# Normed tokens turned for the next pass: DMA transposes of two fp16 parts in place of TensorE transposes

## The chip, the cores and the metric

The kernel runs on one core of a Trainium2 chip. The metric is the device time of one execution in microseconds; the time of a version is the median of its runs. The engines are TensorE (PE, with its weight loads as PEld), VectorE (DVE), ScalarE (ACT), GpSimd (POOL) and SyncE (SP), whose queue issues all DMAs here.

## The reference

There are 64 graphs of 128 nodes with 512 features in fp32. Two masked attentions with 8 heads of 64 follow each other, then a feed-forward block and two more norms:

```python
eq, nk, nv = lin(x, n2e_q), lin(x, n2e_k), lin(x, n2e_v)
edges = ln(attn(eq, nk, nv, adj^T) + x, norm1)
nq, ek, ev = lin(x, e2n_q), lin(edges, e2n_k), lin(edges, e2n_v)
nodes = ln(x + attn(nq, ek, ev, adj), norm2)
h = gelu(lin(nodes, ffn_w1))                      # 512 -> 2048
y = ln(nodes + lin(h, ffn_w2), norm3)             # 2048 -> 512
out = layernorm(x + y)
```

attn(q, k, v, mask) is softmax(q k^T / 8 where the mask is above 0) v, head by head; ln(t, g, b) is (t - mean) / sqrt(var + 1e-5) * g + b over the 512 features.

## The kernel before

The work goes in groups of four graphs (GB = 4, 512 tokens). Attention makes two passes over 16 groups, groups 0 to 15 for the edges and 16 to 31 for the nodes; then the feed-forward pass goes over 16 groups. Every fp32 operand of a projection is held as a high and a low part (x_hi, x_lo), and a product is three matmuls.

A group of attention is four steps, u = 0 to 3. Each engine has its own program, written out by hand in `body(g, parity, before, own, after)`, and the engines meet through semaphores, each executing its list strictly in order. A step of the **PE** (L930 on) is: the keys and the queries of head pair u (24 matmuls), `weigh` of an earlier unit (40 small matmuls of turned probabilities with values, into `out_bank`), a block of values (12 matmuls), and the scores of the unit (12 matmuls). A *unit* is a head pair of the group, 8 score matrices of 128 x 128.

The softmax of a unit goes around DVE and ACT. DVE takes the maxima (`mask_and_maximum`, L760, 8 instructions), ACT the exponentials (`exponentials`, L520) and the high fp16 part (`probabilities_high`, L527), DVE the low part (`probabilities_low`, L769, two instructions), and SP turns both with two DMA transposes (`turn_probabilities`, L377 and L380). Behind p_lo DVE makes the low parts of keys and queries (L741, L744, L749), for which ACT made the high ones (L507 to L514), and then `add_weighed` (L684 to L706): the weighed values, divided by the row sums, are added to the residual tokens into `total[parity]` (L697), with the statistics of the norm (L702, and L706 once a group). Only then does DVE take the maxima of the next unit. Scores wait for q_lo.

**The end of a group's norm, where the change is.** When all four units of group g are added, POOL makes the inverse spread (`inverse_spread`, L608 and L610), and in the next group DVE centres the tokens in place at u = 2 (`centre`, L678, four instructions between v_rest and p_lo). The next pass needs the tokens with features on the partitions, times gain plus shift. So the PE transposes each graph's 128 x 512 tokens into the one bank `turn_bank` (`turn`, L837, four transposes against an identity matrix), and ACT copies it with gain and shift to `turned` (`copy_turned`, L477, four instructions), from where SP stores it (`store_turned`, L386). The four turns of group g-1 are spread over the steps: b = 0 and b = 1 at u = 2 (the second in the middle of a block of values), b = 2 at u = 3, b = 3 at u = 0 of the next group. A turn waits until ACT has copied the one before. In pass 2 the centred tokens are also stored as they are (`store_tokens`, L391).

POOL's list per group is: the middle and low parts of the values (`value_low`, L621 and L623, four times, each after DVE's v_rest of the block, L736), the low part of the next source (`split_source`, L636, four), the value bias onto the residual tokens (`add_bias`, L641, four), `inverse_spread`, and in pass 2 the low part of the next queries (`split_queries`, L630, four). SP's list per group has the loads (source, tokens, adjacency, in pass 2 queries), the eight transposes of probabilities, and the stores.

The first group of the feed-forward pass does the last group's turns: `attention["turn"]` and its fellows at chunks c = 8 to 11, with its weights loaded piece by piece meanwhile.

## Time and profile before

| | us |
|---|---|
| median of 3 runs | 2919.3 (2918.19 to 2920.08) |
| the profiled execution, its own time | 2920.29 |
| its span, first to last instruction | 2918.5 |
| PE busy / PEld busy | 2862.3 (98%) / 2396.2 |
| DVE busy | 1744.8 (60%) |
| ACT busy | 1551.6 (53%) |
| POOL busy | 1094.2 (37%) |
| mean granted PE clock, share of 2.4 GHz | 0.994 |

The shares are of the whole span, of which the attention passes take about the first half. In that half DVE and ACT are far busier than the mean says, since the feed-forward pass needs little of them. A chain of waits follows the last instruction back to what released it. A timeline gives start, duration, engine, line and operation; instructions of a kind that follow each other are merged with "xN", and an instruction that waits for a resource after it was started shows as a longer one.

### The profile page before, as it was taken

The page shows a single profiled execution, that of the slowest core. Times are in us where ns is not written, and L with a number is a line of the kernel's source. Part 1 is how long each engine was busy: PE and PEld are TensorE (multiplying, and loading weights), DVE is VectorE, ACT ScalarE, POOL GpSimd, SP SyncE. Part 2 cuts the span into 40 slices and gives each one's busy share as a digit, 9 for nine tenths or more (in the row PEclk, how much of TensorE's full clock was granted, in tenths as well). Part 3 has the DMA queues.
Part 4 walks back from the last instruction along what each step waited for, and adds up shares of the span by engine and source line. Part 5 has one row for each costly group of instructions (what it writes and reads, how often), then busy time and mean ns, then how long its engine had stood idle before and what let it go on. Part 6 is the DMA issues. An engine that isn't in the chain of part 4 may idle for free.

```text
span 2918.5 us, 50564 instructions
## 1 busy us (share of the span) xinstructions
PE 2862.3 (98%) x17920; PEld 2396.2 (82%) x17920; DVE 1744.8 (60%) x5684; ACT 1551.6 (53%) x4138; POOL 1094.2 (37%) x995
## 2 busy tenths in 40 slices
PE   9999999999999999999989999999999999999997
PEld 7888888888788888888868888888888888888886
DVE  7888888888888888888863233332233332233333
ACT  6777777777778787887854222222222222222221
POOL 3443434434355454654513322233321233321233
PEclk9999999999999999999999999999999999999998
DMA  7555555555567666766653110111110101110101
GB/s 200 121 123 124 123 121 120 115 132 119 139 164 173 161 167 161 180 172 162 163 146 122 58 53 34 43 43 57 57 57 29 52 34 57 57 57 29 67 6 58
DMA packets 488013, 296.08 MB, mean 101 GB/s; under 512 B 278912, under 2 KB 410112, under 8 KB 487808
## 3 DMA queue, kind: packets, MB, share of 16 engines
q1 hardware_dynamic: 487808, 293.49, 38.5%
q8 instruction: 111, 1.82, 0.2%
q14 instruction: 94, 0.77, 0.1%
HBM read 159.21 MB, written 67.11 MB: 78 GB/s over the span
## 4 chain that ended last, share of the span: by engine, by line
PE 94%; ACT 2%; DVE 2%; issue 1%; DMA 0%; SPq 0%; POOLq 0%; POOL 0%; DVEq 0%; ACTq 0%
PE proj L871 34%; PE proj L1320 24%; PE score L1334 12%; PE proj L1334 12%; PE score L922 6%; PE att_out L855 5%; PE att_turn L837 2%; ACT turned L477 1%; ACT att_probs L520 0%; DMA ffn_weight_raw<-in_w 0%; DVE normed L697 0%; DVE ffn_stats L1217 0%; DMA att_weight_v_raw<-in_n2e_v_w 0%; DVE att_p_lo L769 0%; DVE att_stats L702 0%
## 5 line engine op out<-in xcount | busy, mean ns | idle before, releaser
L1253 DVE TENSOR_TENSOR hidden_lo<-hidden,hidden_hi 128x512 fp32r<-128x512 f32 x256 | 186.9, 730 | 936.0 <-ACT hidden_hi L1105 936.0
L1112 ACT ACTIVATE hidden<-proj,ffn_bias 128x512 f32<-128x512 f32 x256 | 176.6, 690 | 996.7 <-PE proj L1320 996.6
L520 ACT ACTIVATE att_probs<-att_probs,att_minus_max 128x128 f32<-128x128 f32 x1024 | 397.3, 390 | 87.0 <-DVE att_minus_max L760 87.0
L769 DVE TENSOR_TENSOR att_p_lo<-att_probs,att_p_hi 128x512 f16<-128x512 f32 x256 | 212.3, 868 | 150.7 <-ACT att_p_hi L527 150.7
L1172 POOL TENSOR_TENSOR source_lo<-source_raw,source_hi 128x512 fp32r<-128x512 f32 x60 | 79.4, 1324 | 449.6 <-ACT source_hi L1123 449.6
L760 DVE CUSTOM_DVE_ANT_0 att_probs<-score,att_mask 128x128 f32<-128x128 f32 x1024 | 225.8, 285 | 34.7 <-PE score L922 34.2
L621 POOL CAST att_v<-att_v_rest 128x512 bf16<-128x512 f32 x128 | 95.6, 747 | 400.6 <-DVE att_v_rest L736 400.6
L477 ACT ACTIVATE turned<-att_turn,att_shift,att_gain 128x128 f32<-128x128 f32 x512 | 192.9, 458 | 69.9 <-PE att_turn L837 69.9
L871 PE MATMUL proj<-weight_v_hi,source_hi 128*128 128x512 f32 x512 | 216.4, 423 | 10.0 <-DVE weight_v_lo L718 7.2
L636 POOL TENSOR_TENSOR source_lo<-source_raw,source_hi 128x512 fp32r<-128x512 f32 x128 | 163.3, 1298 | 131.9 <-ACT source_hi L543 131.9
L871 PE MATMUL proj<-source_hi,weight_k_hi 128*128 128x512 f32 x512 | 201.6, 394 | 2.3 <-DVE weight_k_lo L718 2.3
L871 PE MATMUL proj<-weight_v_hi,source_lo 128*128 128x512 f32 x512 | 202.6, 396 | 0.0
L871 PE MATMUL proj<-weight_v_lo,source_hi 128*128 128x512 f32 x512 | 201.3, 393 | 0.0
L871 PE MATMUL proj<-source_lo,weight_k_hi 128*128 128x512 f32 x512 | 201.1, 393 | 0.0
L871 PE MATMUL proj<-source_hi,weight_k_lo 128*128 128x512 f32 x512 | 199.9, 390 | 0.0
L1320 PE MATMUL proj<-source_hi,w_lo 128*128 128x512 f32 x512 | 199.2, 389 | 0.0
L1320 PE MATMUL proj<-source_hi,w_hi 128*128 128x512 f32 x512 | 199.2, 389 | 0.0
L1320 PE MATMUL proj<-source_lo,w_hi 128*128 128x512 f32 x512 | 199.2, 389 | 0.0
L520 ACT ACTIVATION_READ_ACCUMULATOR att_probs<-att_probs,att_minus_max 128x1 f32 x1024 | 191.8, 187 | 0.0
L641 POOL TENSOR_TENSOR att_tokens<-att_tokens,bias_row 128x512 f32<-128x512 f32 x128 | 182.5, 1426 | 0.3 <-DMA att_tokens<-in_x 0.3
L855 PEld LDWEIGHTS att_out<-att_v,att_pt_hi 128*128 128x128 f16 x3072 | 149.0, 98 | 33.5 <-issue 33.2
L855 PE MATMUL att_out<-att_v,att_pt_hi 128*128 128x64 bf16 x3072 | 164.1, 193 | 0.0
(148 smaller groups left out, 8256.9 us busy)
## 6 DMA issues: line engine op xcount, KB each, us to landing
att_tokens<-in_x SPq DMA_DIRECT2D x128, 256.0 KB, 3.2
edges_t<-turned SPq DMA_DIRECT2D x64, 256.0 KB, 2.7
source_raw<-edges_t SPq DMA_DIRECT2D x16, 1024.0 KB, 6.0
att_query_raw<-in_x_t SPq DMA_DIRECT2D x16, 1024.0 KB, 7.5
nodes_t<-turned SPq DMA_DIRECT2D x64, 256.0 KB, 2.9
source_raw<-nodes_t SPq DMA_DIRECT2D x16, 1024.0 KB, 6.1
normed<-nodes SPq DMA_DIRECT2D x16, 1024.0 KB, 5.6
ffn_weight_raw<-in_x SPq DMA_DIRECT2D x16, 1024.0 KB, 8.1
```

Source lines behind the costliest of these rows:

```text
L477: last = nc.scalar.activation(turned[:, b % 2, c, :], turn_bank[:, c * P:(c + 1) * P], ACT.Identity, bias=shift_column[own][:, c:c + 1], s ...
L520: nc.scalar.activation(probs[:, j, :], probs[:, j, :], ACT.Exp, bias=minus_max[:, j:j + 1], scale=-1.0, accum_out=row_sum[:, side, j:j + 1 ...
L641: nc.gpsimd.tensor_tensor(pair(tokens, u), pair(tokens, u), bias_v[:, u * P:(u + 1) * P].rearrange("p (o d) -> p o d", o=1).to_broadcast([ ...
L760: nc.vector.tensor_tensor_reduce(out=probs[:, 4 * h + j, :], in0=score_bank[h][:, j * P:(j + 1) * P], in1=mask[:, 2 * h + j // 2, :], scal ...
L769: nc.vector.tensor_tensor(p_lo[:, 4 * h:4 * h + 4, :], probs[:, 4 * h:4 * h + 4, :], p_hi[:, 4 * h:4 * h + 4, :], ALU.subtract).then_inc(p ...
L855: last = nc.tensor.matmul(out, p, value, start=(i == 0), stop=(i == len(products) - 1))
L871: last = nc.tensor.matmul(bank[:], stationary, moving, start=(c == 0 and i == 0), stop=(c == C - 1 and i == 2))
L922: last = nc.tensor.matmul(score_bank[h][:, 2 * i * P:2 * (i + 1) * P].rearrange("p (s j) -> p s j", s=2), q, k, start=(n == 0), stop=(n == 2))
L1112: nc.scalar.activation(hidden[:, c % 2, :], up_bank[c % 2][:], ACT.Gelu, bias=bias_1[:, c:c + 1]).then_inc(activated, 1)
L1253: nc.vector.tensor_tensor(hidden_lo[:, c % 2, :], hidden[:, c % 2, :], hidden_hi[:, c % 2, :].bitcast(F32), ALU.subtract).then_inc(hidden_ ...
L1320: last = nc.tensor.matmul(up_bank[c % 2][:], w, s, start=(i == 0), stop=(i == len(products) - 1))
L1334: last = nc.tensor.matmul(down_bank[b][:], h, w, start=(c == 0 and i == 0), stop=(c == FC - 1 and i == 2))
```

## The change

The centred tokens are split on POOL into two fp16 parts, two graphs at a time (q = 0, 1), SP turns each part with a DMA transpose, ACT writes high part times gain plus shift, and DVE adds low part times gain. The turned parts lie in the room of `gain_row` and `shift_row`, which are loaded later. PE transposes, the identity matrix and `turn_bank` are gone. Centring moves from DVE to ACT, for which POOL makes -mean x rstd (`shift_by_mean`), and it stays at u = 2 and 3.

```diff
+    def turn_tokens(sp, g, q):
+        n = 2 * g + q
+        wait(sp, turned_whole, n)
+        sp.wait_ge(token_hi_ready, n + 1)
+        sp.dma_start_transpose(turned_hi..., token_hi[:]...).then_inc(token_hi_turned, 16)
+        sp.wait_ge(token_lo_ready, n + 1)
+        sp.dma_start_transpose(turned_lo..., token_lo[:]...).then_inc(token_lo_turned, 16)
...
+    def centre(act, g, parity, graphs):
+        act.wait_ge(mean_scaled, 2 * g + 2)
+        for b in graphs:
+            data = total[parity][:, b, :]
+            nc.scalar.activation(data, data, ACT.Identity, bias=shift_by_mean[:, b:b + 1], scale=rstd[:, b:b + 1]).then_inc(centred, 1)
+
+    def scale_turned(act, g, q):
+        n = 2 * g + q
+        own = g // NG
+        act.wait_ge(token_hi_turned, 16 * (n + 1))
+        wait(act, turned_out, 16 * n)
+        for c in range(C):
+            nc.scalar.activation(turned[:, c, :, :], turned_hi[:, :, c, :], ACT.Identity, bias=shift_column[own][:, c:c + 1],
+                                 scale=gain_column[own][:, c:c + 1]).then_inc(turned_high, 1)
...
+    def split_tokens(pool, g, parity, q):
+        n = 2 * g + q
+        pool.wait_ge(centred, GB * g + 2 * q + 2)
+        wait(pool, token_hi_turned, 16 * n)
+        wait(pool, token_lo_ready, n)
+        data = total[parity][:, 2 * q:2 * q + 2, :]
+        nc.gpsimd.tensor_copy(token_hi[:], data).then_inc(token_hi_ready, 1)
+        pool.wait_ge(token_hi_ready, n + 1)
+        wait(pool, token_lo_turned, 16 * n)
+        nc.gpsimd.tensor_tensor(token_lo[:], data, token_hi[:], ALU.subtract).then_inc(token_lo_ready, 1)
...
-    def centre(dve, g, parity):
-        dve.wait_ge(rstd_ready, g + 1)
-        for b in range(GB):
-            data = total[parity][:, b, :]
-            nc.vector.tensor_scalar(data, data, moments[:, b, 0:1], rstd[:, b:b + 1], ALU.subtract, ALU.mult).then_inc(centred, 1)
+    def complete_turned(dve, g, q):
+        n = 2 * g + q
+        own = g // NG
+        dve.wait_ge(token_lo_turned, 16 * (n + 1))
+        for c in range(C):
+            dve.wait_ge(turned_high, C * n + c + 1)
+            last = nc.vector.scalar_tensor_tensor(turned[:, c, :, :], turned_lo[:, :, c, :], gain_column[own][:, c:c + 1],
+                                                  turned[:, c, :, :], ALU.mult, ALU.add)
+        last.then_inc(turned_whole, 1)
...
-    def turn(pe, g, parity, b):
-        pe.wait_ge(centred, GB * g + b + 1)
-        wait(pe, turned_copied, GB * g + b)
-        for c in range(C):
-            last = nc.tensor.transpose(turn_bank[:, c * P:(c + 1) * P], total[parity][:, b, c * P:(c + 1) * P], identity[:])
-        last.then_inc(turned_ready, 1)
```

In the bodies: ACT has `scale_turned(g - 2, 0)` at u = 0, `scale_turned(g - 2, 1)` and `centre(g - 1)` of two graphs at u = 2, of the other two at u = 3. POOL has `split_tokens(g - 2, 1)` after the first half of `split_source`, and `split_tokens(g - 1, 0)` after the token add of u = 3. DVE has `complete_turned(g - 2, 0)` at the end of u = 0 and `complete_turned(g - 2, 1)` at the end of u = 2. In the feed-forward pass centring comes at chunk 4, the turned pairs at chunks 6 and 8, and the loads of the node gain and shift rows go behind them; the stores between the passes take 512 KB each.

DVE at u = 2 of a group in pass 1, before. The rows run from the rest of the values (v_rest) to the statistics; the maxima stand ahead of them.

```order
L736 TENSOR_TENSOR att_v_rest<-proj,att_v_1 128x512
L678 TENSOR_SCALAR att_even_sum<-att_even_sum,att_moments,att_rstd 128x512 x4
L769 TENSOR_TENSOR att_p_lo<-att_probs,att_p_hi 128x512 x2
L741 SCALAR_TENSOR_TENSOR att_k_lo<-proj,att_bias_k,att_k_hi 64x512
L744 SCALAR_TENSOR_TENSOR att_k_lo<-proj,att_bias_k,att_k_hi 64x512
L749 SCALAR_TENSOR_TENSOR att_q_lo<-proj,att_bias_q,att_q_hi 128x512
L684 RECIPROCAL att_row_inverse<-att_row_sum 128x8
L697 SCALAR_TENSOR_TENSOR normed<-att_out,att_row_inverse,att_tokens 128x64 x8
L702 BN_STATS att_stats<-normed 128x6 x4
```

The same stretch of the list in the change.

```order
L786 TENSOR_TENSOR att_v_rest<-proj,att_v_1 128x512
L819 TENSOR_TENSOR att_p_lo<-att_probs,att_p_hi 128x512 x2
L791 SCALAR_TENSOR_TENSOR att_k_lo<-proj,att_bias_k,att_k_hi 64x512
L794 SCALAR_TENSOR_TENSOR att_k_lo<-proj,att_bias_k,att_k_hi 64x512
L799 SCALAR_TENSOR_TENSOR att_q_lo<-proj,att_bias_q,att_q_hi 128x512
L735 RECIPROCAL att_row_inverse<-att_row_sum 128x8
L747 SCALAR_TENSOR_TENSOR normed<-att_out,att_row_inverse,att_tokens 128x64 x8
L752 BN_STATS att_stats<-normed 128x6 x4
L727 SCALAR_TENSOR_TENSOR turned<-shift_row,att_gain,turned 128x256 x4
```

Centring (L678) has left the place between v_rest and p_lo, and four additions of low parts (L727, 256 columns) now stand between the statistics and the next maxima; at u = 0 four more stand in the same place.

POOL from the start of a group, pass 1, before.

```order
L621 CAST att_v_0<-att_v_rest 128x512
L623 TENSOR_TENSOR att_v_0<-att_v_rest,att_v_0 128x512
L636 TENSOR_TENSOR source_lo<-source_raw,source_hi 128x512 x2
L641 TENSOR_TENSOR att_tokens<-att_tokens,bias_row 128x4x128
L621 CAST att_v_0<-att_v_rest 128x512
L623 TENSOR_TENSOR att_v_0<-att_v_rest,att_v_0 128x512
```

And in the change.

```order
L662 CAST att_v_0<-att_v_rest 128x512
L664 TENSOR_TENSOR att_v_0<-att_v_rest,att_v_0 128x512
L677 TENSOR_TENSOR source_lo<-source_raw,source_hi 128x512 x2
L648 CAST att_token_hi<-att_even_sum 128x1024
L651 TENSOR_TENSOR att_token_lo<-att_even_sum,att_token_hi 128x1024
L682 TENSOR_TENSOR att_tokens<-att_tokens,bias_row 128x4x128
L662 CAST att_v_0<-att_v_rest 128x512
L664 TENSOR_TENSOR att_v_0<-att_v_rest,att_v_0 128x512
L677 TENSOR_TENSOR source_lo<-source_raw,source_hi 128x512 x2
```

Between the sources' low parts and the token add there are now a cast and a subtraction of 1024 columns; a second such pair stands after the token add of u = 3.

SP at the end of a group of pass 2 and the start of the next, before.

```order
L377 DMA_TRANSPOSE att_pt_hi<-att_p_hi 128x8x128
L380 DMA_TRANSPOSE att_pt_lo<-att_p_lo 128x8x128
L386 DMA nodes_t<-turned 128x4x128
L391 DMA nodes<-normed 128x4x512
L369 DMA att_tokens<-in_x 128x4x128
L421 DMA att_adj<-in_adj_nodes 128x512
L430 DMA att_query_raw<-in_x_t 128x4x512
L377 DMA_TRANSPOSE att_pt_hi<-att_p_hi 128x8x128
L380 DMA_TRANSPOSE att_pt_lo<-att_p_lo 128x8x128
```

And in the change, where `gain_row` and `shift_row` are the turned parts.

```order
L381 DMA_TRANSPOSE att_pt_hi<-att_p_hi 128x8x128
L384 DMA_TRANSPOSE att_pt_lo<-att_p_lo 128x8x128
L403 DMA nodes_t<-turned 128x4x256
L392 DMA_TRANSPOSE gain_row<-att_token_hi 128x8x128
L396 DMA_TRANSPOSE shift_row<-att_token_lo 128x8x128
L409 DMA nodes<-normed 128x4x512
L373 DMA att_tokens<-in_x 128x4x128
L441 DMA att_adj<-in_adj_nodes 128x512
L450 DMA att_query_raw<-in_x_t 128x4x512
L381 DMA_TRANSPOSE att_pt_hi<-att_p_hi 128x8x128
L384 DMA_TRANSPOSE att_pt_lo<-att_p_lo 128x8x128
```

Two transposes of tokens, of which the second waits for POOL's subtraction, now stand ahead of the token store, the loads and the probabilities' next two transposes.

## Rows read from the trace of the kernel before

**Rows 1.** The page, part 4: the chain that ended last, by line.

```profile
PE proj L871 34%; PE proj L1320 24%; PE score L1334 12%; PE proj L1334 12%; PE score L922 6%; PE att_out L855 5%; PE att_turn L837 2%; ACT turned L477 1%; ACT att_probs L520 0%; DMA ffn_weight_raw<-in_w 0%; DVE normed L697 0%; DVE ffn_stats L1217 0%; DMA att_weight_v_raw<-in_n2e_v_w 0%; DVE att_p_lo L769 0%; DVE att_stats L702 0%
```

**Rows 2.** Chain in order of time, pass 1: start us, us, what.

```profile
498.44 0.48 PE att_turn L837 x4
...
526.64 5.46 PE proj L871 x24
...
537.57 5.47 PE proj L871 x24
...
544.22 0.48 PE att_turn L837 x4
```

**Rows 3.** Timeline of DVE, pass 1: start us, us, engine, line, operation.

```profile
503.56 0.28 DVE L760 CUSTOM_DVE_ANT_0 att_probs<-score,att_mask 128x128 f32<-128x128 f32 x1
...
507.68 2.41 DVE L769 TENSOR_TENSOR att_p_lo<-att_probs,att_p_hi 128x512 f16<-128x512 f32 x2 [1.76 <-ACT att_p_hi L527]
...
514.90 0.27 DVE L760 CUSTOM_DVE_ANT_0 att_probs<-score,att_mask 128x128 f32<-128x128 f32 x1
...
519.02 1.84 DVE L769 TENSOR_TENSOR att_p_lo<-att_probs,att_p_hi 128x512 f16<-128x512 f32 x2 [1.23 <-ACT att_p_hi L527]
...
526.10 0.29 DVE L760 CUSTOM_DVE_ANT_0 att_probs<-score,att_mask 128x128 f32<-128x128 f32 x1 [0.34 <-PE score L922]
...
530.24 1.31 DVE L769 TENSOR_TENSOR att_p_lo<-att_probs,att_p_hi 128x512 f16<-128x512 f32 x2 [1.76 <-ACT att_p_hi L527]
...
533.91 1.63 DVE L697 SCALAR_TENSOR_TENSOR att_even_sum<-att_out,att_row_inverse,att_tokens 128x64 f32<-128x64 f32 x8
...
537.00 0.29 DVE L760 CUSTOM_DVE_ANT_0 att_probs<-score,att_mask 128x128 f32<-128x128 f32 x1
...
539.29 4.03 DVE L678 TENSOR_SCALAR att_even_sum<-att_even_sum,att_moments,att_rstd 128x512 f32<-128x512 f32 x4
...
549.34 0.28 DVE L760 CUSTOM_DVE_ANT_0 att_probs<-score,att_mask 128x128 f32<-128x128 f32 x1
```

**Rows 4.** DVE waits, windows 100:700 and 860:1480: us, times, longest.

```profile
DVE att_probs L760 <- PE score L922: 4.0, 12, 0.4
...
DVE att_probs L760 <- PE score L922: 22.4, 26, 1.0
```

**Rows 5.** Timeline of POOL beside rows 3.

```profile
507.80 1.74 POOL L641 TENSOR_TENSOR att_tokens<-att_tokens,bias_row 128x512 f32<-128x512 f32 x1
...
522.11 2.55 POOL L636 TENSOR_TENSOR source_lo<-source_raw,source_hi 128x512 fp32r<-128x512 f32 x2 [2.40 <-ACT source_hi L543]
...
537.19 0.23 POOL L608 TENSOR_SCALAR att_spread<-att_moments 128x4 f32<-128x4 f32 x1
...
551.77 0.61 POOL L621 CAST att_v<-att_v_rest 128x512 bf16<-128x512 f32 x1 [8.73 <-DVE att_v_rest L736]
```

**Rows 6.** Timelines of DVE and POOL in the last group of the feed-forward pass.

```profile
2901.56 0.75 DVE L1197 SCALAR_TENSOR_TENSOR normed<-normed,ffn_moments,turned 128x512 f32<-128x512 f32 x1
...
2901.61 0.78 POOL L1147 TENSOR_SCALAR ffn_spread<-ffn_moments 128x1 f32<-128x1 f32 x1 [0.88 <-DVE ffn_moments L1219]
```

**Rows 7.** Groups by form: busy us, mean ns (feed-forward pass, then pass 1).

```profile
L1203 DVE SCALAR_TENSOR_TENSOR normed<-normed,ffn_rstd,ffn_weight_raw 128x512 f32<-128x512 f32 x64 | 44.0, 745 | 0.0
...
L477 ACT ACTIVATE turned<-att_turn,att_shift,att_gain 128x128 f32<-128x128 f32 x210 | 79.2, 457 | 35.6 <-PE att_turn L837 35.6
...
L543 ACT CAST source_hi<-source_raw 128x512 fp32r<-128x512 f32 x52 | 29.4, 616 | 0.0
```

**Rows 8.** Busy time by engine, clock, DMA share in pass 2.

```profile
860.00:1480.00 620.00, 614.47 (x4973) 521.05 (x4972) 530.27 (x2017) 499.30 (x1513) 332.36 (x296) 1.00 0.68 165
```

**Rows 9.** DMA issues: what, count, KB each, median us to landing.

```profile
att_query_raw<-in_x_t SPq DMA_DIRECT2D x16, 1024.0 KB, 7.5
...
att_pt_hi<-att_p_hi SPq DMA_TRANSPOSE x128, 3.2
```

**Rows 10.** Chain in order of time, from pass 2 into the feed-forward pass.

```profile
1496.30 1.23 SPq L380
```

191 lines of the change are left out of this document (103 added, 88 removed).

## Prediction

> **What bounds the kernel now.** I read the page first: the chain that ended last runs over PE, with att_turn 2% and the ACT copies of the turned bank 1% [rows 1]. So the transposes that this change takes from TensorE lie on the path, and the prize is worth measuring. The chain in order of time shows a group in the first pass from 498.44 to 544.22, 45.78 us, and the step from 526.64 to 537.57, which has no turn in it, takes 10.93 us [rows 2]. Four such steps would be 43.72, so all that hangs on the turns (four bursts of 0.48 us or less, and a wait for the ACT copy of the first before the second) is 45.78 - 43.72 = 2.06 us a group.
>
> Then I asked how near the next engine is. A step on VectorE (DVE) goes from the first maximum of one unit (L760) to that of the next, and it is a closed cycle: maxima, exponentials on ACT, p_hi on ACT, p_lo on DVE, k_lo, q_lo, add_weighed, and only then the next maximum. The maxima that open u=0 to u=3 and the next group stand at 514.90, 526.10, 537.00 and 549.34, the one before at 503.56: steps of 11.34 (u=3), 11.20 (u=0), 10.90 (u=1), 12.34 (u=2), in all 45.78 [rows 3]. In the first pass DVE waited for a score only 4.0 us in 600, or 0.3 us a group; in the second 22.4 us in 620, or 1.7 us a group [rows 4]. **DVE's cycle is as long as PE's chain in pass 1 and 1.7 us shorter in pass 2.** PE has the chain because it never stops, but 2.06 us less of PE is only gained if DVE's cycle gets shorter too.
>
> **What DVE's cycle consists of.** Undisturbed, it is the u=1 step: 526.10 to p_lo at 530.24 is 4.14 us, of which DVE waits 1.76 for ACT; the whole is 10.90. The other steps have p_lo disturbed: 11.34 less 2.41 - 1.31 is 10.24, and 11.20 less 1.84 - 1.31 and less the 0.34 of waiting for scores is 10.33; so an undisturbed step is 10.3, and u=1 has the four aggregates of the norm on top, 0.6 [rows 3]. At 507.68, beside the 2.41, POOL's token add at 507.80 takes 1.74 where this size takes 1.28 (half of 2.55 at 522.11): the first p_lo runs, POOL waits for its end, then the second p_lo waits for the end of POOL's instruction (509.54) [rows 3, 5]. The same shows for the kind of instruction that the change adds, a scalar_tensor_tensor with both tensors in SBUF: POOL's spread of one column starts at 2901.61, inside L1197's 2901.56 to 2902.31, and takes 0.78 us where 128x4 takes 0.23 [rows 5, 6]. So two SBUF inputs on DVE and a reading POOL instruction exclude each other, each for the whole of the other, and when DVE issues such instructions in a row, a waiting POOL gets in between.
>
> The Trainium skill, "SBUF — State Buffer", section "SBUF: two separate sides", calls this pair of ports an exclusive lock held for the whole instruction. No row here has a POOL instruction longer than 1.74 us, so what a 128x1024 one does is not shown; by that rule it would block for its whole length.
>
> **The change, part by part.**
> - PE: 16 transposes a group gone, 2.06 us a group of room [rows 2]. No time comes of it while DVE's cycle is longer.
> - DVE, removed: centring, 4 instructions, 4.03 us at 539.29, but 1.76 of it lay in the wait for p_hi. The u=2 step is 12.34, against 10.3 undisturbed: 2.0 off the cycle in pass 1 [rows 3].
> - DVE, added: eight scalar_tensor_tensor of 256 columns, four at the end of u=0 and four at the end of u=2, where there is no wait to hide them (the order above). 512 columns of this form take 745 ns, and 64 columns follow each other at 1.63/8 = 0.204 us [rows 3, 7]. For 256 that gives at least 0.33 (half of p_lo's 1.31/2) and at most 0.204 + 192 x 0.745/512 = 0.48 us; I take 0.41, in the middle, so 1.64 for four and 3.3 a group, with 2.6 and 3.9 as bounds.
> - ACT: 16 copies of 128 columns at 457 ns go, 7.3 us; 4 centrings of 512 columns, at 616 ns or a little more, and 8 scalings of 256, between the two, at about 0.5, come, 6.5 [rows 7]. ACT sits in the cycle only up to q_hi, and this work stands behind q_hi, so I cost it at nothing; its bounds (5.5 and 7.4) give the same.
> - POOL, added a group: two casts and two subtractions of 128x1024. 512 columns cost 0.61 (L621) and 1.28 (L636) [rows 5]; so 1.2 and 2.5, 7.4 a group, and some 0.5 for the two new 128x4 instructions. POOL's own time is there (332 us busy of 620 in pass 2, [rows 8]); what counts is where it blocks DVE.
> - SP and DMA: four transposes more, two 512 KB stores in place of four of 256 KB. A transpose lands 3.2 us after the start of its issue, which takes 1.23 of SP [rows 9, 10]: 5 us of issue more a group of 45.78, in which SP issues eight today and mostly waits. DMA is busy 0.68 of pass 2 [rows 8]. I cost it at nothing in pass 1, the cover being that a turned pair is used most of a step later; what it costs where that cover is gone is the third rival.
>
> **The sum for a group of pass 1**, with m for the first maximum of a step. That a subtraction of 2.5 us blocks for its whole length, as those of 1.28 do, is my choice; if it let go after 1.28, the sum would be 2 us a group less, which the range holds.
> - u=0: 10.3, p_lo delayed by value_low as today +0.54 (1.84 against 1.31, [rows 3]). POOL ends source_lo near m+9.7 (as at 524.66, [rows 5]) and now starts the cast and the subtraction at once. DVE reaches the four new instructions at m+10.8: one runs at 10.9, the subtraction takes 11.35 to 13.8, the second follows, POOL's token add takes 14.25 to 15.55, then the last two. Next m at 16.3, 5.1 above today's 11.2.
> - u=1: 10.9, as today: POOL's work falls where DVE reads PSUM.
> - u=2: without centring p_lo comes at m+4.14, just when the token add for u=3 is due: +1.2 (the 507.68 pattern). centre on ACT ends near m+9.7, POOL casts to 10.9 and subtracts to 13.3; DVE at m+11.6 waits 1.7, then 1.6 of its own. 15.0, against 12.3.
> - u=3: 11.3, as today.
> Together 53.5, or **7.7 us a group more**. In pass 2 POOL also makes query_lo (four of 1.3 us) before the tokens' parts; walked the same way the blocking moves from u=2 to the next u=0, where value_low and source_lo get between DVE's four, and the period comes to 53 to 54 as well. 30 groups have the whole of it: 30 x 7.7 = 231 us.
>
> Beyond the groups: at the end of pass 2 the last tokens but one are turned between the last units' probabilities and the first feed-forward weights, which the chain goes through (it follows SP there, at 1496.30, to the load of a weight, [rows 10]). Two issues 2.5, landing 1.9, ACT and DVE 3.4, a store 0.6: +8 us. Four turns fewer in the first feed-forward group, -1.4. Sum: 2920.3 (the profiled execution; its span is 2918.5) + 231 + 8 - 1 = 3158; the median of the runs is 1.0 lower. **I predict 3157 us.**
>
> **Rivals.**
> - The blocking stays as it is today (1.7 us a group), since the new instructions meet POOL less than I walked: 4 x 10.3 + 0.6 + 3.3 + 1.7 = 46.8, 1.0 more a group, 2920.3 + 30 + 7 = 2957. For it: POOL's starts hang on events of ACT and DVE, and a shift of 3 us would part them. Against it: POOL starts its long pair as soon as source_lo ends, in the very microseconds in which DVE gets to its four, every group. Between this and the forecast everything is possible, one blocking being 1.3 to 2.5 us.
> - Faster: the DVE cycle falls below 45.78 us, because the removed centring took its blocking with it and the added four meet nothing. That decides once less than 0.6 us a group is spent on blocking, since 4 x 10.3 + 0.6 + 3.3 = 45.1; then 30 x -0.7 = -20 and the boundary +7 give 2907. If the new instructions cost 0.33 each, or fall into DVE's waits for scores, PE sets the pace at 43.72 and the time is 2920.3 - 62 + 7 - 1 = 2864. For it: pass 2 has 1.7 us a group of slack on DVE. Against it: today's steps already hold 1.7 of blocking with 8 us less POOL work a group and eight fewer DVE instructions of the kind that is blocked.
> - Worse: in pass 2 SP waits for the low part of the tokens (POOL, after query_lo) before it may issue store_tokens, two loads and the 1 MB of queries, and the probabilities' transposes queue behind them. One query load alone lands 7.5 us after issue, more than twice the 3.2 of a transpose [rows 9]; with the store of 1 MB ahead of it the pair would land some 5 us after PE wants it for weigh at u=1 (an estimate: POOL's query_lo and token parts end 18 us into u=3, the 2.5 MB take 7.5 + 3, the pair 3, against 27 to weigh). In the forecast the stretched step covers this; if it does not, 15 x 5 = 75 us on top, 3232.
>
> **Chances.** A measurement of this kernel can tell 0.2%, 6 us. Forecast with its spread (a group at 50 to 55.5): 3050 to 3215, 0.55. Light blocking, 2926 to 3050: 0.24. Faster, 2855 to 2913: 0.11. Within 0.2%: 0.03. Above 3215: 0.07. The range leaves out the faster cases and the top: 2945 to 3240. Slower takes 0.86.
>
> **What would show it.** On the DVE row of a group of pass 1: the two sets of four new instructions, some of them 1.5 to 3 us long where others take 0.5, beside casts or subtractions of 128x1024 on POOL; a group of 50 to 55 us; PE at 80 to 88% with waits before the scores for q_lo; PE's chain share down, DVE's and POOL's up. The forecast is wrong if the new instructions all take about 0.5 us, if a POOL subtraction blocks for less than its length, or if PE still never waits. In pass 2, a wait before weigh that ends with a DMA speaks for the third rival.

## The result, and the profile after

The changed kernel took 3134.2 us (median of 4 runs, 3132.9 to 3135.3) against 2919.7 before (4 runs, 2918.2 to 2920.1): a ratio of 1.0734, 95% interval 1.0721 to 1.0748, 214.6 us slower. I had said 3157 us, in a range from 2945 to 3240.

| | before | after |
|---|---|---|
| profiled execution, us | 2920.3 | 3135.1 |
| its span, us | 2918.5 | 3133.3 |
| mean granted TensorE clock | 0.994 | 0.968 |

The chain that ended last, by engine and by line (the second line is the one that answers to [rows 1]):

```profile
PE 53%; DVE 22%; ACT 12%; DMA 4%; SPq 3%; issue 3%; POOL 3%; DVEq 0%; POOLq 0%; ACTq 0%
PE proj L1361 22%; PE score L1375 11%; PE proj L1375 11%; ACT att_probs L543 8%; PE proj L915 6%; DVE turned L727 4%; DVE att_p_lo L819 4%; DMA att_pt_lo<-att_p_lo 3%; DVE att_even_sum L747 2%; DVE normed L747 2%; DVE att_q_lo L799 2%; POOL att_query_lo L671 2%; DVE att_stats L752 2%; DVE att_k_lo L794 2%; PE att_out L899 2%
```

att_turn is gone from it, and 22% of the chain now runs over DVE, with L727, the new addition of the low part, as its largest DVE line. To see where the time came from I divided the span at four first maxima on the DVE row: that of the first unit, of unit 60 (end of the first 15 groups), of unit 64 (first group of pass 2) and of the last unit; "rest" is from there to the end of the span. The same division is used for every kernel below (us).

| kernel | pass 1, 60 units | next 4 | pass 2, 63 units | rest |
|---|---|---|---|---|
| before | 683.3 | 57.7 | 721.3 | 1430.3 |
| after | 770.6 | 60.1 | 815.8 | 1461.2 |
| difference | 87.3 | 2.4 | 94.5 | 30.9 |

So both attention passes are slower by about the same, and there are 31 us behind them.

**Pass 1.** Timeline of DVE in one group: the first maxima of the steps u=1, 2, 3 and 0 and of the next group's u=1, and the last instructions of u=0.

```profile
430.61 0.28 DVE L810 CUSTOM_DVE_ANT_0 att_probs<-score,att_mask 128x128 f32<-128x128 f32 x1
...
441.39 0.23 DVE L810 CUSTOM_DVE_ANT_0 att_probs<-score,att_mask 128x128 f32<-128x128 f32 x1
...
455.98 0.28 DVE L810 CUSTOM_DVE_ANT_0 att_probs<-score,att_mask 128x128 f32<-128x128 f32 x1
...
467.31 0.28 DVE L810 CUSTOM_DVE_ANT_0 att_probs<-score,att_mask 128x128 f32<-128x128 f32 x1
...
475.45 0.75 DVE L799 SCALAR_TENSOR_TENSOR att_q_lo<-proj,att_bias_q,att_q_hi 128x512 fp32r<-128x512 f32 x1 [0.74 <-ACT att_q_hi L537]
...
478.80 5.14 DVE L727 SCALAR_TENSOR_TENSOR turned<-shift_row,att_gain,turned 128x256 f32<-128x256 f16 x4
...
483.86 0.28 DVE L810 CUSTOM_DVE_ANT_0 att_probs<-score,att_mask 128x128 f32<-128x128 f32 x1
```

The steps are 10.78 (u=1), 14.59 (u=2), 11.33 (u=3) and 16.55 (u=0). Over all groups of pass 1 from the third they average 10.78, 14.57, 11.34 and 15.52: 52.2 us, where rows 3 gave 45.78 [rows 3]. The four additions in this u=0 took 5.14 us. POOL at the same time:

```profile
478.48 1.05 POOL L648 CAST att_token_hi<-normed 128x1024 f16<-128x1024 f32 x1
...
479.61 2.21 POOL L651 TENSOR_TENSOR att_token_lo<-normed,att_token_hi 128x1024 f16<-128x1024 f32 x1
...
481.78 1.48 POOL L682 TENSOR_TENSOR att_tokens<-att_tokens,bias_row 128x512 f32<-128x512 f32 x1
```

The u=0 shown is one of two long ones. In the other eleven of these 13 groups it takes 15.3 to 15.4 us (15.34 in the group before, where the additions take 4.64). Between 100 and 700 us the granted TensorE clock was at 1.2 GHz in 13 stretches, eleven of 3.4 us and two of 6.8, and the two of 6.8 reach into the two long steps. One stretch of each kind; the third number from the end is the share of 2.4 GHz:

```profile
412.78:416.19 3.41, 3.41 (x14) 3.31 (x15) 3.34 (x22) 0.60 (x3) 0.00 (x0) 0.50 1.27 212
...
463.98:470.80 6.82, 6.03 (x20) 5.36 (x21) 6.04 (x32) 3.60 (x18) 0.54 (x1) 0.50 1.03 231
```

Each of the two begins in or right behind a wait of PE of 3.5 us for q_lo. In the longer one PE's projections were still slow at the start of u=0, q_lo waited 0.74 us for q_hi (the row at 475.45), and the additions met more of POOL's list. That the clock makes these 1.2 us is read from the rows and not tested; twice 1.2 is little of the 87.

Where nothing disturbs it an addition takes 0.48 us. Its durations over pass 1 (the view of one tile, nanoseconds min/median/max):

```profile
L727 DVE SCALAR_TENSOR_TENSOR turned<-shift_row,att_gain,turned x92: 468/476/2411, 112.7 to 691.7; 128x256 f32<-128x256 f16 x92
```

The longest, 2411 ns, is the 0.48 plus most of a subtraction of 2.2 us. What PE had to wait for in pass 1, and in pass 2 (windows 100 to 700 and 860 to 1450 us; us in total, times, longest):

```profile
PE score L964 <- DVE att_q_lo L799: 65.1, 29, 3.7
...
PE att_out L899 <- DMA att_pt_lo<-att_p_lo: 55.9, 11, 6.6
```

Before, DVE waited for PE's scores [rows 4] and PE only 3.8 us for the copies of its turns; now PE waits for q_lo, the DVE instruction that comes last before the scores. In pass 1 PE is busy 533.4 of 600 us, at a mean granted clock of 0.96 of the 2.4 GHz level; the row behind it is from the feed-forward pass:

```profile
100.00:700.00 600.00, 533.40 (x4048) 442.81 (x4047) 516.76 (x1758) 408.50 (x1197) 299.18 (x274) 0.96 0.56 126
...
2000.00:2300.00 300.00, 300.00 (x1303) 244.33 (x1302) 85.40 (x176) 79.03 (x124) 84.50 (x75) 1.00 0.16 54
```

**Pass 2.** SP's own row at a change of groups (issue time and its length):

```profile
1103.04 1.24 SPq L392 DMA_TRANSPOSE gain_row<-att_token_hi  x1
...
1105.59 1.23 SPq L396 DMA_TRANSPOSE shift_row<-att_token_lo  x1
...
1109.35 1.09 SPq L450 DMA_DIRECT2D att_query_raw<-in_x_t  x1
...
1110.62 2.92 SPq L381 DMA_TRANSPOSE att_pt_hi<-att_p_hi  x1
...
1113.65 3.93 SPq L384 DMA_TRANSPOSE att_pt_lo<-att_p_lo  x1
```

and DVE a little later:

```profile
1109.13 4.66 DVE L727 SCALAR_TENSOR_TENSOR turned<-shift_row,att_gain,turned 128x256 f32<-128x256 f16 x4 [0.75 <-DMA shift_row<-att_token_lo]
...
1119.65 1.40 DVE L819 TENSOR_TENSOR att_p_lo<-att_probs,att_p_hi 128x512 f16<-128x512 f32 x2 [3.57 <-DMA att_pt_lo<-att_p_lo]
```

SP stood at the transpose of the tokens' low part until POOL had made it, then issued a store, two loads and the 1 MB of queries in a row, and 1.3 us behind that load the transposes of the probabilities. These took 2.92 and 3.93 us to issue where 1.23 is normal [rows 10], and the next p_lo waited 3.57 us for the DMA that reads its tile.

### The profile page after: what moved, and what is told of

It reads as the page before. It is cut to its first block, busy times and chain, and to the rows that moved or that the text cites. A ratio compares the mean times of both kernels' runs of the same rounds, so it can differ in the third digit from the quotient of the medians.

```text
span 3133.3 us, 50024 instructions
## 1 busy us (share of the span) xinstructions
PE 2908.8 (93%) x17408; PEld 2393.6 (76%) x17408; DVE 1868.0 (60%) x5812; ACT 1575.4 (50%) x4010; POOL 1312.1 (42%) x1187
## 4 chain that ended last, share of the span: by engine, by line
PE 53%; DVE 22%; ACT 12%; DMA 4%; SPq 3%; issue 3%; POOL 3%; DVEq 0%; POOLq 0%; ACTq 0%
PE proj L1361 22%; PE score L1375 11%; PE proj L1375 11%; ACT att_probs L543 8%; PE proj L915 6%; DVE turned L727 4%; DVE att_p_lo L819 4%; DMA att_pt_lo<-att_p_lo 3%; DVE att_even_sum L747 2%; DVE normed L747 2%; DVE att_q_lo L799 2%; POOL att_query_lo L671 2%; DVE att_stats L752 2%; DVE att_k_lo L794 2%; PE att_out L899 2%
## 5 line engine op out<-in xcount | busy, mean ns | idle before, releaser
L819 DVE TENSOR_TENSOR att_p_lo<-att_probs,att_p_hi 128x512 f16<-128x512 f32 x256 | 236.3, 961 | 232.9 <-ACT att_p_hi L550 183.3
L899 PE MATMUL att_out<-att_v,att_pt_hi 128*128 128x64 bf16 x3072 | 177.6, 199 | 78.2 <-DMA att_pt_lo<-att_p_lo 76.2
L899 PEld LDWEIGHTS att_out<-att_v,att_pt_hi 128*128 128x128 f16 x3072 | 159.2, 102 | 116.3 <-issue 110.6
L964 PE MATMUL score<-att_k_hi,att_q_hi 128*128 128x256 f32 x512 | 155.4, 304 | 89.4 <-DVE att_q_lo L799 89.4
L727 DVE SCALAR_TENSOR_TENSOR turned<-shift_row,att_gain,turned 128x256 f32<-128x256 f16 x256 | 222.4, 928 | 16.1 <-DMA shift_row<-att_token_lo 15.7
L915 PE MATMUL proj<-source_hi,weight_k_hi 128*128 128x512 f32 x512 | 208.4, 407 | 3.5 <-DVE weight_k_lo L768 3.4
L662 POOL CAST att_v<-att_v_rest 128x512 bf16<-128x512 f32 x128 | 78.0, 610 | 283.6 <-DVE att_v_rest L786 282.1
```

What stands on the lines that cost most here:

```text
L727: last = nc.vector.scalar_tensor_tensor(turned[:, c, :, :], turned_lo[:, :, c, :], gain_column[own][:, c:c + 1], turned[:, c, :, :], ALU.m ...
L819: nc.vector.tensor_tensor(p_lo[:, 4 * h:4 * h + 4, :], probs[:, 4 * h:4 * h + 4, :], p_hi[:, 4 * h:4 * h + 4, :], ALU.subtract).then_inc(p ...
L899: last = nc.tensor.matmul(out, p, value, start=(i == 0), stop=(i == len(products) - 1))
L915: last = nc.tensor.matmul(bank[:], stationary, moving, start=(c == 0 and i == 0), stop=(c == C - 1 and i == 2))
L964: last = nc.tensor.matmul(score_bank[h][:, 2 * i * P:2 * (i + 1) * P].rearrange("p (s j) -> p s j", s=2), q, k, start=(n == 0), stop=(n == 2))
```

## Experiments

The theory going in (**A**): DVE's closed cycle is the bound and became longer, by additions that no wait hides and by POOL's instructions of 128x1024 that hold them up. Rivals: **B**, the four more DMA transposes; **C**, the order of SP's queue in pass 2; **D**, ACT's longer list. All kernels in one table, divided as above; the ratio is to runs of before on the same chip.

| kernel | median us | ratio (95%) | pass 1 | next 4 | pass 2 | rest |
|---|---|---|---|---|---|---|
| b_centre_act | 2982.2 | 1.021 (1.0193 to 1.0227) | 696.4 | 55.9 | 748.1 | 1453.4 |
| b_dma_only | 2919.0 | 0.9994 (0.9985 to 1.0004) | 683.5 | 55.4 | 721.5 | 1430.3 |
| a_no_complete | 3014.5 | 1.0321 (1.0304 to 1.0339) | 670.2 | 55.6 | 801.0 | 1460.4 |
| a_short_split | 3033.9 | 1.0384 (1.0367 to 1.0401) | 708.7 | 57.2 | 779.9 | 1461.6 |
| a_query_late | 3115.7 | 1.0671 (1.0653 to 1.0689) | 769.7 | 61.6 | 795.1 | 1461.8 |
| a_add_early | 3050.5 | 1.0447 (1.0430 to 1.0464) | 697.3 | 57.6 | 807.2 | 1461.7 |
| a_halves | 3142.0 | 1.0763 (1.0746 to 1.0779) | 769.0 | 60.4 | 821.9 | 1461.6 |
| b_spread | 2918.1 | 0.9993 (0.9983 to 1.0003) | 676.0 | 56.9 | 727.9 | 1430.7 |
| b_spread_bias | 2931.2 | 1.0041 (1.0026 to 1.0055) | 684.1 | 57.4 | 733.3 | 1431.8 |
| c_early_late | 3020.1 | 1.0344 (1.0328 to 1.0360) | 697.1 | 58.7 | 773.1 | 1463.2 |
| c_pool_gated | 2917.0 | 0.9990 (0.9981 to 0.9999) | 654.1 | 55.4 | 719.1 | 1461.1 |
| c_gated_512 | 2891.5 | 0.9901 (0.9885 to 0.9918) | 654.5 | 54.0 | 715.2 | 1438.5 |

**b_dma_only.** The kernel before, with the transposes of two tiles of zeros added:

```diff
             turn_probabilities(sp, C * g)
+            if not below(g, 2):
+                turn_tokens(sp, g - 2, 1)
...
                 store_turned(sp, g - 1, before, 2)
+                turn_tokens(sp, g - 1, 0)
```

> The kernel before, all its work kept, and four more DMA transposes of 128 x 1024 fp16 per group out of two tiles of zeros, at the places in SyncE's list where the change has its own. Theory A: SyncE and the DMA queue have room in the first pass; there nothing is lost, in the second pass at most 2 us a group for the transposes of the probabilities that come behind them: 2915 to 2950 us. Rival B (the transposes by DMA and their issue are the cost, as late probabilities and late loads): most of the 215 us appear here, 3050 us or more.

No loss in any stretch, pass 2 included. Rival B is out: SP, the queue and the DMA engines carry four more transposes a group for nothing, as long as SP never has to wait for their data. SP's row at a change of groups in pass 2 (tokens' transposes, the load of the queries, the probabilities' transpose):

```profile
1117.37 1.26 SPq L392 DMA_TRANSPOSE gain_row<-att_token_hi  x1
...
1118.75 1.26 SPq L396 DMA_TRANSPOSE shift_row<-att_token_lo  x1
...
1122.51 1.11 SPq L447 DMA_DIRECT2D att_query_raw<-in_x_t  x1
...
1125.22 1.77 SPq L381 DMA_TRANSPOSE att_pt_hi<-att_p_hi  x1
```

The load of the queries goes out 2.7 us ahead of the probabilities' transposes here, 1.3 us in the changed kernel.

**a_no_complete.** The changed kernel, complete_turned empty, its waits given to the last scaling:

```diff
-        dve.wait_ge(token_lo_turned, 16 * (n + 1))
-        for c in range(C):
-            dve.wait_ge(turned_high, C * n + c + 1)
-            last = nc.vector.scalar_tensor_tensor(turned[:, c, :, :], turned_lo[:, :, c, :], gain_column[own][:, c:c + 1],
-                                                  turned[:, c, :, :], ALU.mult, ALU.add)
-        last.then_inc(turned_whole, 1)
...
-        sp.wait_ge(turned_whole, 2 * g + q + 1)
+        sp.wait_ge(turned_high, C * (2 * g + q + 1))
```

> The changed kernel without VectorE's adding of the low part (the stored tokens turned for the next pass are those of the high part alone; everything else, the low part's making and transposes included, runs). Theory A: VectorE's loop falls to 41.8 us a group plus some blocking by GpSimd, TensorE's 43.7 us without turns is the bound: 44 to 46 us a group, 2860 to 2925 us in all. Rival B (DMAs): still 3080 us or more. Rival D (ScalarE's list): 3000 us or more.

Pass 1 is what A says: 44.8 us a group (10.77, 11.66, 10.87, 11.54 from u=0 to u=3), 13 us less than before for the pass. The additions cost 770.6 - 670.2 = 100 us there. But the total misses A's 2860 to 2925, for pass 2 hardly gained: its steps are 11.1, 18.0, 11.0 and 11.0. The step of 18 us has this on SP and among DVE's waits (window 860 to 1450):

```profile
1101.42 1.19 SPq L450 DMA_DIRECT2D att_query_raw<-in_x_t  x1
...
1102.79 2.35 SPq L381 DMA_TRANSPOSE att_pt_hi<-att_p_hi  x1
...
1105.25 4.27 SPq L384 DMA_TRANSPOSE att_pt_lo<-att_p_lo  x1
```

```profile
DVE att_p_lo L814 <- DMA att_pt_lo<-att_p_lo: 92.2, 11, 9.6
```

With the additions gone SP reaches the load of the queries as late as ever (POOL's parts set that), and the probabilities come earlier. The low part that SP turns at 1105.25 was complete at 1095.64; until 1102.6 SP was at the tokens' two transposes, a store of 1 MB, two loads and the queries. Then the two transposes take 2.35 and 4.27 us to issue, and p_lo waits up to 9.6 us. Of the 8.5 us that it waits in this step the slow issue is some 4 (6.6 in place of 2.5, an estimate from these rows), the rest is SP's late start. C is real, and additions and SP's list had been covering each other. The 3014.5 us lie where D was to show too (3000 or more), but the steps speak against D: three of the four in pass 2 take 11.0 or 11.1 us, and the fourth waits for a DMA.

**a_short_split.** POOL's two instructions on 32 columns in place of 1024, the rest of the two parts left at zero:

```diff
-        nc.gpsimd.tensor_copy(token_hi[:], data)
+        nc.gpsimd.tensor_copy(token_hi[:, :, 0:16], data[:, :, 0:16])
...
-        nc.gpsimd.tensor_tensor(token_lo[:], data, token_hi[:], ALU.subtract)
+        nc.gpsimd.tensor_tensor(token_lo[:, :, 0:16], data[:, :, 0:16], token_hi[:, :, 0:16], ALU.subtract)
```

> The changed kernel with GpSimd's cast and subtraction done on 16 columns of each of two graphs (32 in place of 1024 per partition), the rest of the two parts left at zero; all waits, transposes, scalings and additions stay. Theory A with its two halves: the additions undisturbed cost 4 x 0.47 us at two steps of four, the blocking (about 3 us a group by the difference of the steps) goes: 46 to 48 us a group in the first pass, 2945 to 3020 us in all. If blocking is nothing and all is the additions: over 3080 us. If all is blocking: under 2930 us. Rival B (DMAs): over 3080 us.

47.6 us a group in pass 1 (12.81, 10.77, 12.70, 11.36). The additions in pass 1, same view as above:

```profile
L729 DVE SCALAR_TENSOR_TENSOR turned<-shift_row,att_gain,turned x100: 465/476/936, 112.9 to 686.2; 128x256 f32<-128x256 f16 x100
```

So 770.6 - 708.7 = 62 us of pass 1 are GpSimd's two long instructions, with the 2.4 us of the two long steps, which this kernel does not have. The additions without the long pair are 12.81 - 10.77 = 2.04 us at u=0 (the second number from the kernel without them), where POOL's token add still holds up the first for 0.93, and 12.70 - 10.87 = 1.83 at u=2, 50 us in 13 groups. These are more than the 100 us together because in a_no_complete the long pair still meets p_lo: its u=1 is 11.66 where this kernel has 10.77. The total is 14 us above the range because pass 2 again gave less than pass 1.

**a_halves.** The same two instructions, one graph at a time:

```diff
-        nc.gpsimd.tensor_copy(token_hi[:], data).then_inc(token_hi_ready, 1)
+        for b in range(2):
+            last = nc.gpsimd.tensor_copy(token_hi[:, b, :], data[:, b, :])
+        last.then_inc(token_hi_ready, 1)
```

and the subtraction likewise.

> The changed kernel with GpSimd's cast and subtraction each done in two instructions of one graph (512 columns) in place of one of 1024. Theory (one GpSimd instruction holds a VectorE instruction with SBUF sources until it ends, and VectorE gets in between two): the longest addition falls from 2.4 us to 1.3 us or so, each of the two steps of four additions gains up to 1 us: 3070 to 3125 us. Rival (VectorE does not get in between, or GpSimd only ends later by its extra start-up): 3125 to 3145 us.

```profile
L731 DVE SCALAR_TENSOR_TENSOR turned<-shift_row,att_gain,turned x92: 467/1380/1515, 112.9 to 688.9; 128x256 f32<-128x256 f16 x92
```

Half of the expectation came true: the longest addition fell from 2.4 to 1.5 us. But the time, 3142.0 us, is the rival's. Over the whole run 124 of the 256 additions took more than 0.7 us where 94 had, and their sum is the same, 237.0 us against 237.5. One DVE instruction gets in between two pieces, and the next one waits for the next piece: in the group at 425 us three additions in a row take 1.39, 1.38 and 1.51 us, where the changed kernel has 2.37, 1.50 and 0.47. No time is won. The Trainium skill, "SBUF — State Buffer", section "SBUF: two separate sides", has the port pair locked for the whole of an instruction; the trace agrees, up to 2411 ns beside a subtraction of 2.2 us and up to 1405 ns beside pieces of 1.15 to 1.38 us. The additions of 1.5 us lie beside source_lo and the token add (1.3 to 1.5 us), as they did before.

**b_centre_act.** The kernel before with the centring on ACT:

```diff
                 if u == 2 and not starts(g):
+                    centre(act, g - 1, 1 - parity, range(0, 2))
                     copy_turned(act, g - 1, before, 0)
                     copy_turned(act, g - 1, before, 1)
                 if u == 3:
+                    if not starts(g):
+                        centre(act, g - 1, 1 - parity, range(2, 4))
```

> The kernel before with the centring alone moved to ScalarE as in the change (GpSimd makes minus the mean times the inverse spread), VectorE's four centring instructions gone. Theory A (VectorE's loop from maxima to maxima became longer than TensorE's work, by the low part's additions and by GpSimd's splits that hold them up): nothing to lose here, TensorE stays the bound with some 45.8 us a group, so 2905 to 2925 us; a little faster if centring had been in VectorE's way at the third step. Rival D (ScalarE's longer list makes the exponentials late): 2950 us or more, since centring is about half of what ScalarE gained.

62 us slower, in the range that I had given D, but not in D's way: p_lo waits for ACT at most 1.8 us, as before. PE and ACT in the third step:

```profile
413.30 0.66 PE L845 MATMUL att_turn<-att_identity,normed 128*128 128x128 f32 x4 [0.30 <-ACT normed L476]
```

```profile
412.44 1.51 ACT L476 ACTIVATE normed<-normed,att_shift_by_mean,att_rstd 128x512 f32<-128x512 f32 x2
...
414.00 1.51 ACT L484 ACTIVATE turned<-att_turn,att_shift,att_gain 128x128 f32<-128x128 f32 x4
```

Here PE itself waits for the centred tokens, 0.3 us in each of two steps (25 times and 7.5 us in 600, before never), beside the 0.3 for the copy that it had waited before; it was the bound, so this counts, and the third step takes 12.72 us in place of 12.33, the fourth 11.79 in place of 11.35. In pass 2, which has 27 of the 62 us, ACT's centring also makes the high parts of the queries later: POOL starts their low part 8.8 us into u=3 in place of 7.4, its list behind that comes later, p_lo at u=0 takes 3.3 us for 2.5, and that step 12.32 for 11.42. The changed kernel has no turns on PE, so this part of it is not rival D for that kernel: in its pass 1 p_lo waits for ACT no longer than before (1.8 us on average at u=1, 2 and 3), and q_lo 1.5 us in 600. In its pass 2 POOL starts the queries' low part 8.55 us into u=3 instead of 7.35; what this costs there wasn't taken apart. But 23 of the 62 us lie in "rest", with nothing there but one centring moved. That pointed at something else, below.

**a_query_late** and **a_add_early**, one move each:

```diff
-            if own == 1 and after == 1:
-                sp.wait_ge(query_ready, C * (g + 1 - NG))
-                sp.dma_start(query_raw[:], query_view[:, :, bass.ds((g + 1 - NG) * GT, GT)]).then_inc(query_in, 16)
...
             turn_probabilities(sp, C * g)
+            if own == 1 and after == 1:
+                sp.wait_ge(query_ready, C * (g + 1 - NG))
+                sp.dma_start(query_raw[:], query_view[:, :, bass.ds((g + 1 - NG) * GT, GT)]).then_inc(query_in, 16)
```

> The changed kernel with one SyncE command of the second pass moved: the 1 MB load of the next group's queries goes out behind the next two pairs of transposes of the probabilities, not 1.3 us ahead of one. Theory C (in the second pass the transposes of the probabilities wait in the DMA queue behind that load, because SyncE first waited for GpSimd's parts): VectorE's wait for the transposed low probabilities (3.3 us where 1.76 us is normal) goes, the second step falls from 12.9 to 10.9 us, 15 groups: 3134 - 30 = 3090 to 3115 us. Rival (the wait comes from late parts on GpSimd, or from the store and the token transposes themselves): within 10 us of 3134.

The second step of pass 2 fell from 12.94 to 11.29 us, not to the expected 10.9, and pass 2 by 20.7 us; 3115.7 is 0.7 above my range. C holds, with this size for the place of the load alone: the probabilities' two transposes still stand behind the 1 MB store of tokens and take 2.00 and 3.09 us to issue (at 1104.36 and 1106.47).

```diff
+                if u in (1, 3) and not below(g, 2):
+                    complete_turned(dve, g - 2, u // 2)
                 if not first:
                     probabilities_low(n, 0)
...
-                if u in (0, 2) and not below(g, 2):
-                    complete_turned(dve, g - 2, u // 2)
```

> The changed kernel with VectorE's four additions of a half moved one step later, between the value rest and the low probabilities, where VectorE otherwise waits 1.76 us for ScalarE's high probabilities. Theory A (undisturbed they take 1.9 us and are hidden there; the rest is GpSimd's blocking): each of the two steps loses most of its 2 us, the blocked part (about 3 us a group) stays or goes as GpSimd is busy in that place: 45.5 to 49 us a group, 2960 to 3060 us in all. If the additions' cost did not depend on their place: within 15 us of 3134.

Pass 1 goes from 52.2 to 46.9 us a group; the place of the additions alone is worth 73 us there. What is left is blocking, DVE and then POOL:

```profile
443.63 3.84 DVE L727 SCALAR_TENSOR_TENSOR turned<-shift_row,att_gain,turned 128x256 f32<-128x256 f16 x4
...
447.39 1.28 DVE L819 TENSOR_TENSOR att_p_lo<-att_probs,att_p_hi 128x512 f16<-128x512 f32 x2
```

```profile
441.32 2.16 POOL L651 TENSOR_TENSOR att_token_lo<-normed,att_token_hi 128x1024 f16<-128x1024 f32 x1
...
443.44 1.30 POOL L682 TENSOR_TENSOR att_tokens<-att_tokens,bias_row 128x512 f32<-128x512 f32 x1
...
444.68 0.81 POOL L662 CAST att_v<-att_v_rest 128x512 bf16<-128x512 f32 x1
```

**c_early_late.** Both moves.

> The changed kernel with both moves together: the additions in VectorE's wait for the high probabilities, and the load of the queries behind the transposes of the probabilities. Theory: the first pass keeps the 46.9 us a group of the first move; in the second pass, where the first move left a second step of 18.4 us with 7 us of waits for DMA in it, the step falls to 12.5 to 13.5 us: 3050 - 15 x 5.3 = 2960 to 2990 us. If those waits come from late parts on GpSimd: 3030 us or more.

3020, outside my range: pass 2 gained 34 us on a_add_early, where I had expected 80. DVE's wait for DMA did go in the main (between 860 and 1450 us 28.5 us in a_add_early, 6.4 here; ACT's fell from 68.5 to 37.3, PE's from 57.2 to 26.1), but the second step still takes 16.4 us, and the row shows why, in pass 2, where POOL has the queries' low part to make too and its whole list runs late and without a gap (DVE, then POOL):

```profile
877.93 6.17 DVE L727 SCALAR_TENSOR_TENSOR turned<-shift_row,att_gain,turned 128x256 f32<-128x256 f16 x4
...
884.15 2.64 DVE L819 TENSOR_TENSOR att_p_lo<-att_probs,att_p_hi 128x512 f16<-128x512 f32 x2
```

```profile
877.65 2.73 POOL L677 TENSOR_TENSOR source_lo<-source_raw,source_hi 128x512 fp32r<-128x512 f32 x2
...
880.32 1.23 POOL L648 CAST att_token_hi<-att_even_sum 128x1024 f16<-128x1024 f32 x1
...
881.64 2.18 POOL L651 TENSOR_TENSOR att_token_lo<-att_even_sum,att_token_hi 128x1024 f16<-128x1024 f32 x1
...
883.78 1.45 POOL L682 TENSOR_TENSOR att_tokens<-att_tokens,bias_row 128x512 f32<-128x512 f32 x1
```

Four additions of 0.48 took 6.17 us, p_lo 2.64 in place of 1.31. So POOL's place in time, not its amount, was next to test.

**c_pool_gated.** POOL waits for the step's p_lo, in three of four steps before anything else and in the fourth behind the values' low part, and makes the tokens' parts ahead of the queries' low part:

```diff
+            wait(pool, p_lo_ready, 2 * C * g)
             value_low(g, parity, 1)
-            split_source(g, parity, range(0, 2))
             if not below(g, 2):
                 split_tokens(pool, g - 2, parity, 1)
-            add_bias(g, 1)
+            split_source(g, parity, range(0, 2))
+            pool.wait_ge(p_lo_ready, 2 * C * g + 2)
             value_low(g, parity, 2)
             split_source(g, parity, range(2, 4))
+            add_bias(g, 1)
             add_bias(g, 2)
...
             value_low(g, parity, 3)
-            if own == 1 and after == 1:
-                split_queries(g + 1)
+            pool.wait_ge(p_lo_ready, 2 * C * g + 4)
             add_bias(g, 3)
             if not starts(g):
                 split_tokens(pool, g - 1, 1 - parity, 0)
+            pool.wait_ge(p_lo_ready, 2 * C * g + 6)
             if not at(g, last_group - 1):
                 value_low(g + 1, 1 - parity, 0)
+            if own == 1 and after == 1:
+                split_queries(g + 1)
```

> The same, and GpSimd's list rearranged: in three of four steps its instructions wait until VectorE has made the low probabilities of the step, and in the second pass the parts come ahead of the queries' low part. Theory (VectorE is held up only in its low probabilities, its additions and other instructions with both sources in SBUF, and 21 to 26 us of GpSimd's work fit beside the rest): both steps of additions come down to 10.9 to 11.2 us, TensorE's 43.7 us is the bound nearly everywhere: 44.0 to 45.0 us a group, 2870 to 2915 us in all, less than before. If GpSimd's list becomes too long in the second pass: 2915 to 2980 us. If VectorE's blocking only moves to other instructions: as c_early_late.

103 us less than c_early_late from the order and the waits of one engine's list, with all of its work kept. Pass 1 is at 43.7 us a group (10.95, 10.90, 11.22, 10.63), 29 us below before for the pass: TensorE's own 43.72 [rows 2]. The total only equals before and is 2 us above my range, because "rest" is still 1461 and pass 2 stays at 45.8 us a group. There one collision is left, as read from the trace and not tested: POOL's token add waits for its load (64.0 us between 860 and 1450 us), so that the subtraction of 1024 columns lands on the additions of u=3, one of which takes up to 2.4 us, and that step takes 12.5. DVE and POOL, from c_gated_512, where these rows are the same:

```profile
419.91 1.67 DVE L733 SCALAR_TENSOR_TENSOR turned<-shift_row,att_gain,turned 128x256 f32<-128x256 f16 x4
...
421.76 1.29 DVE L825 TENSOR_TENSOR att_p_lo<-att_probs,att_p_hi 128x512 f16<-128x512 f32 x2 [0.18 <-ACT att_p_hi L551]
```

```profile
413.96 1.04 POOL L649 CAST att_token_hi<-normed 128x1024 f16<-128x1024 f32 x1
...
415.08 2.16 POOL L652 TENSOR_TENSOR att_token_lo<-normed,att_token_hi 128x1024 f16<-128x1024 f32 x1
...
417.19 2.55 POOL L678 TENSOR_TENSOR source_lo<-source_raw,source_hi 128x512 fp32r<-128x512 f32 x2
...
423.12 0.61 POOL L663 CAST att_v<-att_v_rest 128x512 bf16<-128x512 f32 x1 [3.37 <-DVE att_p_lo L825]
```

The long pair and source_lo end at 419.74, the four additions start at 419.91 and take 1.67, p_lo 1.29, and POOL comes back behind it. In pass 1 no addition takes more than 0.49 us.

**c_gated_512.** One size:

```diff
-            "shift_by_mean": [P, GB],
+            "shift_by_mean": [P, P],
```

> c_pool_gated with one tile's size changed and nothing else: the tile for minus the mean times the inverse spread has 512 bytes a partition (as the identity that it replaces had) where it had 16, so that all tiles allocated behind it, the feed-forward weights and hidden tiles among them, lie again where they lay in the kernel before, and not 496 bytes lower. Theory (the part of the run behind the last maxima, 1430 us in every kernel with the old addresses and 1461 in those with the small tile, 1453 in before with the centring on ScalarE, is longer because TensorE's instructions of 512 columns follow each other at 230 ns in place of 226.5 in the feed-forward pass, and this comes from the tiles' addresses): the feed-forward group takes 87.1 us in place of 88.5, 16 x 1.4 = 23 us less, and up to 10 us more in the attention passes: 2875 to 2897 us. Rival (the slower instructions come from the program around them, not from addresses): 2912 to 2920 us.

2891.5 us, 1.0% less than before and 7.7% less than the changed kernel. "Rest" fell by 22.6 us. The steady part of the feed-forward pass, 300 us with PE never idle, in before and in this kernel:

```profile
2000.00:2300.00 300.00, 300.00 (x1325) 248.51 (x1324) 91.76 (x186) 78.92 (x123) 90.19 (x79) 1.00 0.14 49
```

```profile
2000.00:2300.00 300.00, 300.00 (x1325) 248.39 (x1325) 103.05 (x216) 78.39 (x122) 75.64 (x72) 1.00 0.13 45
```

1325 matmuls of 512 columns in 300 us are 226.4 ns each; the changed kernel's row above has 1303, 230.2 ns, all three at a granted clock of 1.00. The 16-byte tile that took the place of the 512-byte identity tile had moved everything allocated behind it 496 bytes a partition lower (in b_centre_act, which has both, 16 bytes higher). These two moves are 512 bytes apart, and they slow the same forms alike: between 2000 and 2600 us proj<-source_lo,w_hi follows at 233.9 ns in b_centre_act and 234.0 in c_pool_gated, score<-w_lo,hidden_hi at 231.8 in both, and in before and c_gated_512 every form is at 226.6 or 226.7. In pass 2 the 512-column projections follow each other at 230.5 ns in c_pool_gated and 228.8 in c_gated_512, and that pass is 3.9 us shorter; in pass 1 it is 228.3 and 228.6. Which tile it is that must not lie so, and which multiple counts, wasn't tried.

**b_spread** and **b_spread_bias**, the kernel before with its turns one per step:

```diff
-                    if u == 2 and not starts(g):
-                        turn(pe, g - 1, 1 - parity, 0)
+                    if not starts(g):
+                        turn(pe, g - 1, 1 - parity, u - 2)
...
-                if u == 0 and not below(g, 2):
-                    turn(pe, g - 2, parity, 3)
+                if u < 2 and not below(g, 2):
+                    turn(pe, g - 2, parity, u + 2)
```

> The kernel before with its own turns on TensorE, but one graph per step (third, fourth, first, second step) in place of two at the third step, one at the fourth and one at the first. The second turn of the third step then no longer waits 0.3 us for ScalarE's copies and the steps are even: the third falls by about 0.9 us, the second rises by 0.6. Theory (TensorE is the bound, 43.7 us of work a group and 4 x 0.4 to 0.5 us of turns): 45.3 to 45.6 us a group, 2905 to 2920 us in all. If VectorE's loop is the bound at the fourth step (11.35 us, GpSimd's blocking of the low probabilities): no gain, 2915 to 2925 us.

> The same, and GpSimd adds the value bias to the next tokens ahead of the low value parts, so that this SBUF instruction no longer lies beside VectorE's low probabilities at the fourth step (2.4 us there, 1.3 us where GpSimd is idle). Theory (an instruction of GpSimd holds up a VectorE instruction that has both sources in SBUF): the fourth step falls from 11.35 to TensorE's 10.9 to 11.2 us in the first pass, 2 to 8 us less than the kernel with the turns spread alone. Rival (the low probabilities are slow there for another reason, or the blocking only moves to another instruction): within 2 us of it.

The first gains 7.3 us in pass 1 (45.2 a group) and loses 6.6 in pass 2. The gain isn't where I expected it: the third step stays at 12.32 us, and u=0 falls from 11.19 to 10.78. The loss in pass 2 can be read from the trace, though it wasn't tested: ACT now copies a turn ahead of the queries' high parts at u=3, POOL starts their low part 9.7 us into the step in place of 7.4, PE waits 0.5 us a group for it (13 times, before never), and u=0 takes 12.11 us for 11.42. The second kernel also adds the bias of the tokens ahead of the values' low part; it is worse by 13. The token add that I put ahead of the values' low part waits for a DMA, and everything behind it on POOL goes with it:

```profile
448.14 1.30 POOL L640 TENSOR_TENSOR att_tokens<-att_tokens,bias_row 128x512 f32<-128x512 f32 x1 [1.03 <-DMA att_tokens<-in_x]
```

In pass 1 PE now waits four times for the values' low part, up to 2.3 us, and the fourth step is still 11.26: the low part of the values runs beside p_lo there, in the place of the token add (p_lo 2.37 us at 462.38, POOL at 462.71). A list is only improved if the whole of it is placed.

## Why the prediction held, step by step

**The bound.** "2.06 us less of PE is only gained if DVE's cycle gets shorter too" is right, shown from both sides: with DVE's cycle lengthened PE waits for q_lo, and with the cycle brought down (c_pool_gated) exactly those 2 us a group appear in pass 1.

**The additions.** I took 0.41 us each from a range of 0.33 to 0.48, and that was right: one takes 0.48 from start to end, but in a row they follow each other every 0.40, and four take 1.65 to 1.67 where I had 1.64.

**Blocking for a whole instruction.** My choice, and right: a_short_split and a_halves show it. In u=0 I walked to 16.3, measured 15.5 on average (15.3 to 15.4 in eleven groups, 16.5 in the two with the longer stretch at 1.2 GHz); in u=2 15.0, measured 14.57; u=1 10.9 and 10.78; u=3 11.3 and 11.34. Pass 1: 53.5 said, 52.2 measured, from 45.78.

**POOL's sizes.** 1.2 and 2.5 us said, 1.04 and 2.16 measured (medians of pass 1). In u=0 this is some 0.4 of the 1.0 us by which the usual step is shorter than walked; another 0.4 is the token add, which starts as soon as the subtraction ends (at 428.54 in the group before the one shown), and not after one more addition. In u=2 the subtraction ends only 0.1 us earlier than walked (13.2 us into the step for 13.3), and the rest of the step behind it is 1.4 us where I had 1.7.

**ACT at nothing.** Right in pass 1. Its new instructions are dearer than said (scaling 0.59 for 0.5, centring 0.8 for 0.62), and still cost nothing there: in a_no_complete p_lo waits for p_hi no longer than the old 1.76 us. b_centre_act shows that this holds only because PE no longer waits for what ACT centres. In pass 2 ACT's centring makes POOL's query_lo later by 1.2 us, which the forecast didn't have; the longer steps of the changed kernel leave its price unseen.

**Pass 2.** I put it at the same period of 53 to 54 and gave the queue's order as a rival with 75 us on top. Measured 52.0 a group: steps of 16.97, 12.94, 11.82 and 10.24. The mechanism of that rival was there (SP waits for the low part, the 1 MB load goes out just ahead of the probabilities' transposes) but as 2 us of one step, of which moving the load (a_query_late) took back 1.6; the rest was covered by the longer u=0, as the forecast supposed. Where the additions go, its price is 7 us a group.

**The boundary.** +8 us for the end of pass 2 and -1.4 for the first feed-forward group said, 6.6 together. The last kernel, with the old addresses, has 1438.5 - 1430.3 = 8.2 in "rest"; of which parts, I did not look.

**What failed.** The sum had 231 us for 30 groups; the passes gave 87 + 2 + 95 = 184. The term that was mis-sized is the surplus of a group, 7.7 us said against 6.4 in pass 1 and 6.2 in pass 2 (52.0 against 45.8); of the 1.3 us in pass 1, 0.8 are in u=0 and 0.4 in u=2, for the reasons above. And the sum had no loss for the feed-forward pass, where 1461.2 - 1438.5 = 23 us were lost to addresses: a part of the change that looked like bookkeeping, the replacing of one small tile by another, was not priced (in pass 2 it's worth some 4 us more, 719.1 - 715.2). The two cancel in part: 47 too many in the groups, 23 not seen, and 3158 less 3135.1 is 23. That the forecast came so near is partly this luck.

## What to carry to other kernels

Before work goes from an engine on the path to others, ask for the closed cycle that runs beside the path: here DVE's was as long as PE's chain, and every instruction added behind its last wait counted in full, while the same four put into an existing wait of 1.76 us cost nothing where GpSimd was kept away (0.18 us of that wait is left in c_gated_512). GpSimd and VectorE together need a timetable, not a share of busy time: the same 25 us of GpSimd work per group of pass 1 cost 3 us or nothing by its order and a few waits (c_early_late against c_pool_gated). And after any change of tile sizes compare how many matmuls fit in a stretch in which TensorE never stops.

## What the runs showed that I had not expected

- **Matmul spacing follows the SBUF layout.** A small tile of 16 bytes in place of 512 ahead of the others made fp32 matmuls of 512 columns follow each other at 230.2 ns on average and not 226.4, in a pass whose code did not change; restoring the size restored the spacing, 22.6 us of the run. It also fits the 23 us in "rest" of b_centre_act, the one variant of before that has the small tile, and there too 1303 matmuls stand in the 300 us; b_dma_only and the two spread ones lack it and have 1430 to 1432 us and 1325 matmuls.
- **Cutting a blocking instruction in two frees nothing** when the other engine has a row of short ones: one gets in per gap, and the sum of the additions' durations stayed at 237 us.
- **Two costs can hide each other.** Taking the additions away made the second step of pass 2 longer, from 12.9 to 18.0 us, because DVE and ACT were no longer late enough for SP's list.
